# Eight-head attention on one core: low parts of keys and queries on VectorE, and seven of eight key tiles summed on GpSimd

## The reference

```
xn  = group_norm(x) * w + b
qkv = W @ xn + bias                      # keys, queries, values of 8 heads
weight = softmax(q^T k / sqrt(32))       # 1024 x 1024 for each head
a   = v @ weight^T
out = (xn or x) + proj(a)
```

## Time and profile before

| | |
|---|---|
| median of 3 runs | 1812.68 us (1807.4 to 1812.93) |
| profiled execution | 1806.44 us |
| its span, first to last instruction | 1804.6 us |
| TensorE busy | 1640.8 us |
| VectorE, GpSimd, ScalarE busy | 1048.2, 993.7, 904.0 us |
| mean granted TensorE clock | 0.956 |

### The profile page before, as it was taken

One profiled execution on the slowest core, in us unless ns is written; L12 is line 12 of the kernel. 1 busy time (PEld: TensorE's weight loads), 2 busy tenths in 40 slices (PEclk: granted clock), 3 DMA queues, 4 the chain that ended last, 5 costly groups with the idle time before them and its releaser, 6 DMA issues.

```text
span 1804.6 us, 25016 instructions
## 1 busy us (share of the span) xinstructions
PE 1640.8 (91%) x8222; PEld 1007.3 (56%) x8222; DVE 1048.2 (58%) x1643; ACT 904.0 (50%) x1488; POOL 993.7 (55%) x393
## 2 busy tenths in 40 slices
PE   4888969999993889998999999999999999999987
PEld 3767758888882454545545545555455454554532
DVE  3655645454432766765667565666676576756621
ACT  3444324334322156555665556556565566555653
POOL 1222312122103166886688677787688678767885
PEclk7999989999996689999999999999999999999999
DMA  4000000000000333031130330302303123033000
GB/s 144 19 18 18 1 1 1 1 1 1 1 0 24 70 71 69 3 71 31 42 72 1 71 73 16 71 19 59 71 1 72 42 55 71 1 96 72 1 25 24
DMA packets 25005, 67.57 MB, mean 37 GB/s; under 512 B 7200, under 2 KB 8992, under 8 KB 24864
## 3 DMA queue, kind: packets, MB, share of 16 engines
q1 hardware_dynamic: 24864, 65.78, 15.0%
HBM read 7.82 MB, written 4.19 MB: 7 GB/s over the span
## 4 chain that ended last, share of the span: by engine, by line
PE 48%; DVE 8%; issue 5%; POOL 4%; DMA 2%; ACT 1%; SPq 1%; POOLq 0%; DVEq 0%; ACTq 0%
PE psO L894 12%; PE psD L79 11%; PE psD L962 10%; PE psA L987 7%; DVE BNS L1040 6%; PE psD L906 5%; POOL PA L1218 3%; PE psO L987 3%; DMA QS<-MROW 2%; ACT PR L1151 1%; DVE sums_turned L1017 1%; DVE A L1021 1%; SPq L1242 0%; SPq L1244 0%; DVE A L1023 0%
## 5 line engine op out<-in xcount | busy, mean ns | idle before, releaser
L1040 DVE TENSOR_REDUCE BNS<-psD 128x1 f32<-128x512 f32 x1024 | 631.4, 683 | 193.2 <-PE psD L962 193.2
L1218 POOL TENSOR_TENSOR PA<-PA,PR 128x2048 f32<-128x2048 f32 x128 | 586.1, 4579 | 13.9 <-ACT PR L1151 1.7
L1151 ACT ACTIVATE PR<-psA 128x512 f32<-128x512 f32 x688 | 396.1, 607 | 329.5 <-PE psA L987 286.9
L962 PE MATMUL psD<-KS,QS 96*128 96x512 f32 x1024 | 421.3, 445 | 17.4 <-DMA QS<-SL 10.8
L987 PE MATMUL psA<-QS,KS 97*128 97x512 f32 x688 | 295.4, 438 | 38.9 <-DMA QS<-MROW 17.4
L962 PEld LDWEIGHTS psD<-KS,QS 96*128 96x128 f32 x1024 | 199.2, 195 | 139.4 <-DVE BNS L1040 92.2
L1151 ACT ACTIVATE PR<-psO 128x512 f32<-128x512 f32 x336 | 203.7, 606 | 139.2 <-PE psO L987 136.9
L609 POOL TENSOR_SCALAR P<-P,RS 128x1024 f32<-128x1024 f32 x64 | 72.1, 1126 | 365.1 <-DVE RS L348 365.1
L894 PE MATMUL psO<-PR,V 128*32 128x512 f32 x2048 | 246.5, 598 | 0.0
L1218 POOL TENSOR_TENSOR PA<-PR 128x2048 f32<-128x2048 f32 x32 | 146.4, 4576 | 149.0 <-PE psD L962 130.5
L987 PEld LDWEIGHTS psA<-QS,KS 97*128 97x128 f32 x688 | 128.7, 190 | 178.1 <-issue 93.8
(11 more groups left out here) (141 smaller groups left out, 2079.0 us busy)
## 6 DMA issues: line engine op xcount, KB each, us to landing
KS<-SH SPq DMA_DIRECT2D x128, 128.0 KB, 2.4
QS<-SH SPq DMA_DIRECT2D x128, 128.0 KB, 2.5
KS<-SL SPq DMA_DIRECT2D x64, 128.0 KB, 2.5
QS<-SL SPq DMA_DIRECT2D x64, 128.0 KB, 2.5
X<-x SPq DMA_DIRECT2D x4, 1024.0 KB, 7.9
out<-X SPq DMA_DIRECT2D x4, 1024.0 KB, 4.6
KH<-KL SPq DMA_DIRECT2D x8, 128.0 KB, 2.3
QH<-KL SPq DMA_DIRECT2D x8, 128.0 KB, 2.4
```

Source lines behind the costliest of these rows:

```text
L962: mm = e.matmul(full, QS[0:STACK, g, q, tile * PART:(tile + 1) * PART], KS[0:STACK, g, q, h * HALF:(h + 1) * HALF], start=True, stop=True)
L1040: top = e.tensor_reduce(MXH[:, h, q, tile:tile + 1], full, AX.X, ALU.max)
L1151: e.activation(PR[:, J % 4, (s % QUADH) * HALF:(s % QUADH + 1) * HALF], score_bank(s, p), ACT.Exp, scale=scale).then_inc(exp_done, 1)
L1218: e.tensor_tensor(PA[:, :], PR[:, (J - 1) % 4, :] if j == 1 else PA[:, :], PR[:, J % 4, :], ALU.add).then_inc(sum_done, 1)
```

## The change

`DIRECT` goes from 2 to 1: GpSimd makes six adds a half (seven tiles) instead of five, and a z unit has 16 records instead of 24. `PIECES` follows. The low parts leave GpSimd: ScalarE writes the rounded part of a half of K or Q straight from the bank to `SH`, and VectorE computes the low part of that half from the same bank, (bank + bias) - `SH`, one instruction of 128x512. The separate copies and GpSimd's `low` go. VectorE's work is now in the order of `vector_order`: keys and queries stand at their step plus `LOW_LAG` = 1.7. The bank of a key or query unit is given back by VectorE (`given_back`, `bank_free`). SyncE waits for the last low part in VectorE's count (`keys_split`).

```diff
-DIRECT = 2
+DIRECT = 1
+        LOW_LAG = 1.7
...
-            return sum((u in "vwkqKQ") == (engine == "scalar") for u, _, _ in units[:k])
+            return sum((u in "vw") == (engine == "scalar") for u, _, _ in units[:k])
+        def vector_order(units):
+            return sorted((at + LOW_LAG * (u in "kqKQ"), k) for k, (u, at, _) in enumerate(units) if u not in "vw")
+        def given_back(place, r, k):
+            if UNITS[place][k][0] in "vw":
+                return "scalar", base_of("scalar", place, r) + taken(UNITS[place], k + 1, "scalar")
+            return "vector", base_of("vector", place, r) + [j for _, j in vector_order(UNITS[place])].index(k) + 1
...
+        def keys_split(G):
+            M, u = (0, "q") if G == 0 else (G - 1, "Q")
+            place, r = (M, None) if M < 2 else (2 + M % 2, M // 2 - 1)
+            last = max(k for k, x in enumerate(UNITS[place]) if x[0] == u)
+            return given_back(place, r, last)[1]
...
-        PIECES = NT - 1
+        PIECES = NT
...
-                        for j in (NT - 1, NT - 2, NT):
+                        for j in (NT - 1, NT):
...
-                            if j == NT - 2:
+                            if j == NT - 1:
                                 mm.then_inc(av_done, 1)
...
-                            all_taken(place, r, k - BANKS + 1)
+                            bank_free(place, r, k - BANKS)
...
+                        elif u in "kqKQ":
+                            group, gg = (G + 1, 1 - g) if u in "KQ" else (G, g)
+                            which, mv = int(u in "qQ"), slice(i * HALF, (i + 1) * HALF)
+                            e.wait_ge(high_done, 4 * group + 2 * which + i + 1)
+                            bias = par(f"bqk{layers[1]}", 4)[:, 2 * gg + which:2 * gg + which + 1]
+                            e.scalar_tensor_tensor(out=SL[:, which, mv].bitcast(F32R), in0=full, scalar=bias, in1=SH[:, which, mv],
+                                                   op0=ALU.add, op1=ALU.subtract).then_inc(vec_free, 1)
...
-                        if what == "high":
-                            e.drain()
-                            e.activation(SH[:, which, :].bitcast(F32R), SL[:, which, :], ACT.Copy).then_inc(high_done, 1)
-                            return
...
+                                e.activation(SH[:, which, mv].bitcast(F32R), full, ACT.Identity, bias=bias).then_inc(high_done, 1)
...
-                    def low(group, which):
-                        wait(e, high_done, group * 2 + which + 1)
-                        e.tensor_tensor(SL[:, which, :].bitcast(F32R), SL[:, which, :], SH[:, which, :],
-                                        ALU.subtract).then_inc(low_done, 1)
...
-                        e.wait_ge(low_done, 2 * (G + 1))
+                        e.wait_ge(vec_free, keys_split(G))
```

More of the change, by code:

```diff
@@ L868, in eight_heads_in @@
             xn_done, xh_done, xl_done = sem("xn_done" + n), sem("xh_done" + n), sem("xl_done" + n)
-            high_done, low_done, row_dma = sem("qk_high" + n), sem("qk_low" + n), sem("max_row_filled" + n)
+            high_done, row_dma = sem("qk_high" + n), sem("max_row_filled" + n)
             stack_dma = [sem(f"stack_filled{n}_head{q}") for q in range(QUADH)]
@@ L907, in sums, with bank_free @@
                                               start=(j == NT - 1), stop=(j == NT))
-                            if j == NT - 2:
+                            if j == NT - 1:
                                 mm.then_inc(av_done, 1)
                         return mm
[L912 to L916, removed]
+                    def bank_free(place, r, k):
+                        if k < 0:
+                            wait(e, vec_free, base_of("vector", place, r) + k + 1)
+                            return
+                        engine, count = given_back(place, r, k)
+                        wait(e, act_free if engine == "scalar" else vec_free, count)
                     def project(out_ap, column, h):
@@ L953, in unit @@
                             halves_v = [j for j, (name, _, _) in enumerate(UNITS[place]) if name == "v"]
-                            all_taken(place, r, halves_v[i] + 1)
+                            bank_free(place, r, halves_v[i])
                             for n in range(NT // 2):
@@ L964, in unit @@
                         elif u == "T":
-                            all_taken(place, r, k)
+                            bank_free(place, r, k - 1)
                             mm = e.transpose(full[0:QUADH * NT, 0:PART], MX[:, :], ident[:, :])
@@ L1055, in phase @@
                     def phase(P, p, G, g, place, r, layers, proj=None, norm=None, norm_b=None):
-                        events = [(at, 0, k, "unit") for k, (u, at, i) in enumerate(UNITS[place])
-                                  if u not in "vwkqKQ"]
+                        events = [(at, 0, k, "unit") for at, k in vector_order(UNITS[place])]
                         if norm is not None:
@@ L1112, in run @@
                                 stacks_filled(e, G)
[L1113 to L1116, removed]
+                            if u == "v":
+                                e.activation(VT[:, mv], full, ACT.Identity,
+                                             bias=par(f"bv{layers[0]}", 2)[:, g:g + 1]).then_inc(act_free, 1)
+                            else:
+                                bias = par(f"bqk{layers[1]}", 4)[:, 2 * gg + which:2 * gg + which + 1]
+                                e.activation(SH[:, which, mv].bitcast(F32R), full, ACT.Identity, bias=bias).then_inc(high_done, 1)
                     def phase(P, p, G, g, place, r, layers, proj=None, norm=None, norm_b=None):
@@ L1122, in phase @@
                                 step = -int(-at // 1) + 1
-                                if P is not None:
-                                    assert -int(-UNITS[place][k + BANKS][1] // 1) >= step
                                 events.append((step, 0, "unit", k))
-                                if i == 1 and u in "kqKQ":
-                                    events.append((step + 1 if P is not None else step, 1, "high", k))
                         if norm is not None:
@@ L1205, in phase @@
                             input_low(norm, norm_b, layers[2])
-                            for which in range(4):
-                                low(which // 2, which % 2)
                             return
@@ L1225, in phase @@
                                                     ALU.subtract).then_inc(w3_split, 1)
-                            if G is not None and h == 0:
-                                for which in range(2):
-                                    low(G + 1, which)
                     all_phases(e, phase)
```

## The result

The change made the kernel slower: 1885.65 us, median of 4 runs (1883.42 to 1886.92), against 1810.91 for the kernel before, run beside it (4 runs, 1807.40 to 1812.93). The ratio is 1.0422, with a 95% interval of 1.0398 to 1.0446. The forecast was 1878 in 1842 to 1900. The profiled execution took 1883.42 with a span of 1881.6 us: 77.0 more than before, where the sum said 66. The mean granted TensorE clock is 0.943, before 0.956.

The account below looks back on a forecast made before the run. The prediction took TensorE to bound most of the kernel and GpSimd its end. Its terms, -26.1 + 60 + 22.7 + 13.9 - 4.3, gave +66 on 1806.4, so 1873; forecast median 1878 us, range 1842 to 1900.

Parts of the forecast that it names:

- the sum: All terms of the forecast together, over the whole kernel: +66 us on the profiled execution.
- The start: First group: low parts ready 7.8 us earlier on VectorE, some 3.5 given back before the maxima's transfer; -4.3 us.
- The holds: Key and query projections: TensorE waits for banks until VectorE's subtraction, 4.0 us in each of 15 phases; +60 us.
- smaller holds: Rival at the key and query projections: VectorE takes low parts sooner, say 2 us a phase; 1847 us; chance 0.18.
- no effect: Rival for the whole kernel: holds nearly vanish and the rest cancels, 1813 to 1819 us; chance 0.06.
- a gain: Rival for the whole kernel: TensorE's work alone decides and its queue never waits; -25 us, 1788; chance 0.06.
- The middle of a phase: Between a phase's halves: the extra GpSimd add ends before z needs it, 1.3 to 2.9 us left; costs nothing.
- The boundary: Between phases: the first exponential waits for another add, delaying TensorE's fourth score at eleven boundaries; +22.7 us.
- the removed matmuls: Sums units in P = 0 to 14: eight of 24 TensorE records go, 0.87 us a unit, 30 units; -26.1 us.
- the rival of the clock: Rival at eleven boundaries: added idleness drops TensorE to 1.2 GHz, 14 to 19 us more; 1891 to 1896; chance 0.2.
- The last phase: Last phase: GpSimd's adds run end to end, so three more adds of 4.65 us show fully; +13.9 us.
- Signs that were set too low: Expected in the later profile: ScalarE's boundary wait 3 to 5 us, projection phases 78 to 79, last phase near 93.

Follow-up runs that it names:

- lows_only: The changed kernel with DIRECT back at 2: five GpSimd adds a half, low parts on VectorE; 1868.45 us, ratio 1.0348 to the kernel before.
- lag12: The changed kernel with LOW_LAG 1.2 instead of 1.7, so VectorE takes keys and queries earlier; 1837.12 us, ratio 1.0175 to the kernel before.
- adds_only: The kernel before with only the seventh tile added by GpSimd, low parts left on GpSimd; 1830.92 us, ratio 1.0137.
- adds_filled: adds_only with nine unused filler matmuls before the fourth score in phases of even P from 2 on; 1831.10 us, ratio 1.0146 to the kernel before.
- adds_fine: adds_only with a phase's first four tiles waiting only for the add freeing their own buffer; 1812.75 us, ratio 1.0038 to the kernel before.
- the best version: adds_fine with three direct tiles in the last phase, so four GpSimd adds a half there; 1797.78 us, ratio 0.9955 to the kernel before.

## Why the prediction was right

**The sum.** 66 predicted, 77.0 measured. The 11 us between are 1 in the holds, 6 at the boundaries and 4 in the last phase. The step that was off is the clock, a term that the sum had at nothing: it costs 14 us at the boundaries and some 3.6 in the last phase, and waits 8 us smaller than worked out give part of that back.

**The start.** -4.3 predicted, -4.2 measured, and the parts are right: the first maximum of the first group comes 8.2 us earlier (585.77 against 594.01; predicted 7.8), of which 4.0 are given back by the time its transfer goes out (predicted 3.5). That it agrees to 0.1 is luck: that transfer goes out between 637.3 and 640.9 in the nine profiled runs with the old low parts, and between 631.5 and 634.2 in the five with the new.

**The holds.** 15 x 4.0 = 60 predicted; 61 measured, 4.08 a phase. lows_only isolates the part, and lag12 isolates the mechanism. The four waits came where the order put them, Q0's and Q1's to within 0.01 us of 1.83. The rivals of smaller holds, of no effect and of a gain fall with it.

**The middle of a phase.** K0 to z is unchanged in adds_only: the sixth add is hidden, as worked out.

**The boundary and the removed matmuls.** -26.1 + 22.7 = -3.4 predicted for P = 0 to 14; 63.6 less the holds leaves +2.4. That this is near is partly luck, for two errors nearly cancel. The waits are 14.4 us instead of 22.7: where P's first matmuls are slow, TensorE comes late by itself and has less to wait for, which I had allowed for only at the loops' jumps. And the clock costs what the main sum had at nothing: -26.1 + 14.4 = -11.7, so 14.1 us are left for it. The rows find about as much: the 7.0 in the six slow sums units, and 7.7 at the starts of P = 2, 4, 6 and 12, which from the first to the fourth score, the wait taken off, need 7.15 to 8.26 us where they needed 5.60 to 5.62 before. This is the rival of the clock in kind and in size (14 to 19): nine slow boundaries more. Two things differ: half of it falls on the sums, and it takes the place of part of the wait instead of coming on top, so the time lies between the forecast and that rival's 1891. That added idle time is never free, as the rival has it, isn't so: in adds_filled P = 5 and 13 wait 2.02 and 1.92 us for the fourth score and have no slow record at their start or in their sums. adds_fine takes the wait away but not the clock.

**The last phase.** +13.9 predicted for three adds, +17.5 measured. The adds are as they were (4.5 to 4.6 us, end to end); the term was sized without the clock, granted at 0.81 there instead of 0.95. In the chain's rows the two sums of eight records and the closing projection hold 0.86 + 0.53 + 1.34 = 2.7 of the 3.6; the first sums unit and the scores beside the sums hold most of the rest.

**Signs that were set too low.** ScalarE's wait before its first exponential was to be 3 to 5 us; it is 7.4 to 7.9 from P = 1 on, which the prediction's own 3.17 + 4.65 gives. Phases with projections were to take 78 to 79 us and take 79.7 to 81.4, and the last 93, not 97.3.

**Where the expected gain went.** adds_fine has the seventh tile and next to no wait for exponentials at the boundaries. By the removed matmuls alone it would be 26.1 less 12.9 (its last phase, 92.7 against 79.8), 13.2 us faster; its span is 6.8 longer. Most of the 20 us between are in TensorE's own instructions, by line and form of adds_fine:

```profile
L79 PE MATMUL psD<-XH,WH 128*128 128x512 f32 x200 | 72.0, 445 | 10.4 <-POOL XL L1191 10.4
L79 PE MATMUL psD<-XH,WL 128*128 128x512 f32 x200 | 71.1, 441 | 0.0
...
L79 PE MATMUL psD<-XL,WH 128*128 128x512 f32 x200 | 69.2, 430 | 0.0
...
L906 PE MATMUL psD<-PA,ones 128*32 128x512 f32 x256 | 36.1, 637 | 19.1 <-POOL PA L1218 19.1
L906 PE MATMUL psD<-PR,ones 128*32 128x512 f32 x256 | 34.8, 616 | 0.0
```

The same projections (67.5, 66.5 and 65.6 us before), none added, are busy for 12.7 us more. In P = 0 to 14, without the last phase, the ledger closes: TensorE is busy for 10.6 us less instead of 26.1 and idle for 4.6 more, for it still waits for GpSimd in some phases (2.7 before the sums, 3.1 before the statistics). Of the 15.5 us of slower work 12.5 are in the projections and most of the rest in the sums. Thirteen of the fourteen boundaries are slow, twelve at the phase's start. So the removed work came back mostly as slower work. Why the clock should fall at a start where TensorE was idle no longer than before (1.12 us at P = 8 in both) is not shown; no run set that apart.

## What to carry to other kernels

A bank shared between engines comes back when its taker has its *turn*, not when it is able to: four instructions of 0.74 us cost 4.1 us a phase, 3.2 of them because they stood behind a maximum whose matmul was the next in line, and moving them up half a step in the order gave back 48 of 61 us. Lay the two engines' orders side by side before handing a bank to another engine. And before moving work to an engine with idle time, look at its slack at the boundaries: GpSimd was busy for 55% of the span, yet an add of 4.65 us had only some 3 us of room behind the last one, and none in the last phase, where the best version gives it less work rather than more.

## What was unexpected in the hardware

TensorE's clock fell at places where no wait had been added: the start of P = 8 lies behind 1.12 us of idleness in the kernel before and in adds_fine, and is fast in one and slow in the other. The kernel before has five slow boundaries of fourteen; with another add of GpSimd in front of each, all fourteen are slow in adds_only and in the changed kernel and thirteen in lag12, at the phase's start (a pair of projection matmuls in 1.05 us instead of 0.63) or in the sums unit behind the second wait (eight records in 1.96 us instead of 1.04). Taking the second wait away (adds_fine) left thirteen. The length of the wait just before doesn't tell which: in adds_filled the sums behind waits of 1.87 and 2.37 us (P = 3 and 9) ran at 1.2 GHz in part or whole, and those behind 2.02 and 1.92 us (P = 5 and 13) at 2.4. The clock's price has to be read over a whole phase, and over several of them.
